# A two-layer graph attention kernel: when the second layer's softmax centre and weights are made, with deeper mask buffers and one product of the start held back

## The reference, cut to what matters

```python
src, dst = h @ a1, h @ a2
e = src[:, None] + dst[None, :]
e = where(e > 0, e, SLOPE * e)            # 0.01 in layer 0, 0.2 in layer 1
e = where(adj > 0, e, -9e15)
h_prime = softmax(e, axis=1) @ h
x = layernorm(x + h_prime)                # layer 1: h -> Wh = x @ W, and elu(h_prime)
```

## Time and profile before

| what | value |
|---|---|
| time, median of 3 runs | 433.5 us (432.94 to 433.63) |
| the profiled execution, its time | 433.0 us |
| its span, first to last instruction | 431.2 us |
| mean granted TensorE clock | 0.978 |
| PE busy | 397.9 us (92%) |
| DVE busy | 371.6 us (86%) |
| ACT busy | 382.6 us (89%) |
| POOL busy | 270.6 us (63%) |

### The profile page before, as it was taken

How to read it: one execution, slowest core, us unless ns; L and a number is a source line. 1 busy time by engine, 2 the same in 40 slices (tenths; PEclk the granted TensorE clock), 3 DMA queues, 4 the chain that set the end, 5 groups by cost and what they waited for, 6 DMA issues and landing times. The chain is left out here.

```text
span 431.2 us, 11604 instructions
## 1 busy us (share of the span) xinstructions
PE 397.9 (92%) x4372; PEld 385.7 (89%) x4372; DVE 371.6 (86%) x683; ACT 382.6 (89%) x594; POOL 270.6 (63%) x323
## 2 busy tenths in 40 slices
PE   3589999999999999999988999999999999999990
PEld 1478898899999999999887999999999999999980
DVE  4799999798899898998999978888888888888863
ACT  4789995998989898979999989999999999999920
POOL 5654287494967949497583226576766758493941
PEclk9599999999999999999999999999999999999995
DMA  6999959989999999999600000000000000000000
GB/s 123 97 104 104 83 41 91 96 62 101 83 96 99 86 96 74 96 81 91 56 14 2 2 26 2 2 26 2 27 2 24 0 24 0 24 2 26 2 26 16
DMA packets 38844, 21.66 MB, mean 50 GB/s; under 512 B 1808, under 2 KB 38800, under 8 KB 38800
## 3 DMA queue, kind: packets, MB, share of 16 engines
q0 software_dynamic: 33792, 16.78, 50.9%
q1 hardware_dynamic: 3920, 3.25, 2.5%
q10 hardware_dynamic: 1088, 1.05, 0.7%
HBM read 69.30 MB, written 2.10 MB: 166 GB/s over the span
## 5 line engine op out<-in xcount | busy, mean ns | idle before, releaser
L1254 PE MATMUL acc<-wmov,pos 128*128 128x195 bf16 x2016 | 357.0, 248 | 11.4 <-DVE pos L864 9.8
L673 ACT ACTIVATE neg<-srcb,dcol 128x512 int8<-128x512 f32 x512 | 357.0, 1014 | 0.5 <-PE acc L1254 0.3
L1254 PE MATMUL acc<-wmov,neg 128*128 128x195 bf16 x2016 | 357.0, 249 | 0.0
L1254 PEld LDWEIGHTS acc<-wmov,pos 128*128 128x128 fp8e5 x2016 | 198.6, 99 | 18.2 <-DVE pos L864 15.0
L1254 PEld LDWEIGHTS acc<-wmov,neg 128*128 128x128 fp8e5 x2016 | 197.6, 98 | 1.4 <-issue 0.7
L864 DVE SCALAR_TENSOR_TENSOR pos<-mask_t,neg 128x512 uint32<-128x512 uint32 x128 | 106.4, 831 | 23.1 <-PE acc L1254 11.0
L852 DVE SCALAR_TENSOR_TENSOR neg<-mask_t,neg 128x512 uint32<-128x512 uint32 x128 | 103.4, 808 | 10.5 <-ACT neg L673 9.2
L487 POOL DMA_DIRECT2D enc<-in_adj x64 | 49.3, 773 | 12.2 <-PE tb L1170 4.2
L349 POOL TENSOR_TENSOR scr<-scr,acol 128x260 f32<-128x260 f32 x14 | 13.3, 953 | 61.7 <-issue 51.8
L332 POOL TENSOR_TENSOR split<-val,bcol 128x520 f32<-128x520 f32 x15 | 17.6, 1174 | 26.9 <-DVE scr L396 12.2
L880 DVE TENSOR_REDUCE scr<-acc 128x130 f32<-128x390 f32 x60 | 31.6, 557 | 1.6 <-PE acc L1254 0.2
(11 more groups left out here) (138 smaller groups left out, 305.3 us busy)
## 6 DMA issues: line engine op xcount, KB each, us to landing
enc<-in_adj POOLq DMA_DIRECT2D x64, 256.0 KB, 11.5
x_chunks<-in_x ACTq DMA_DIRECT2D x4, 256.0 KB, 5.1
x_rows<-xout SPq DMA_DIRECT2D x8, 128.0 KB, 5.1
resid<-x_rows SPq DMA_DIRECT2D x8, 128.0 KB, 2.1
out<-xout SPq DMA_DIRECT2D x8, 128.0 KB, 1.7
resid<-in_a SPq DMA_DIRECT2D x1, 64.0 KB, 4.0
resid<-in_w SPq DMA_DIRECT2D x2, 16.0 KB, 4.0
att<-in_a SPq DMA_DIRECT2D x2, 0.2 KB, 4.5
```

The costliest lines, as they stand in the source:

```text
L673: ins = nc.scalar.activation(neg[:, k % SR, :, b], srcb[:, q % 2, :], ACT.Sign, bias=dcol[:, layer, c:c + 1])
L1254: ins = nc.tensor.matmul(acc[t][:, side * WC:(side + 1) * WC], m[:, t * P:(t + 1) * P, b], wmov[:, layer, c, side * WC:(side + 1) * WC], s ...
```

## The change

- The centre of layer 1 is the maximum over group 0 alone (`CENTRES = 1`), found in supertile 2 of layer 0. `centre` still cuts at +20, and the input check on the limits stays.
- From then on one group a supertile goes through the chain: group q - 2 is centred at DVE's step 4 of supertile q (step 1 in supertile 7) and exponentiated by ACT after its step 6 (step 4 in supertile 7); group q - 3 is multiplied by POOL after its stage 2, weighed by DVE at step 6 and kept by ACT after step 7, in supertiles 3 to 6. Supertile 7 weighs groups 4 and 5 (steps 4 and 6). Groups 6 and 7 stay in supertile 0 of layer 1.
- In supertiles 3 to 6 POOL's `multiply` stands ahead of the loads of step 3 and of `epilogue_norm`.
- The looks of supertiles 3 to 5 of layer 0 go: three are left in supertile 2, four in supertile 1 of layer 1, and five (before: four) in each of its supertiles 2 to 6.
- SR goes from 4 to 8 and MR from 2 to 4. The room comes from `s_prod` and `d_prod`, which now lie in the part of `mask_t` for supertiles 7 and 6.
- POOL's product for s waits until DVE has done all four products for d.
- The loop covers supertiles 3 to 6, and supertile 2 is written out; one semaphore replaces the pair `w_prod`.

The diff, cut to its core:

```diff
-SR = 4
-MR = 2
+SR = 8
+MR = 4
-EARLY = 5
+CENTRES = 1
-LOOKS = (4, 5)
-LATE_LOOKS = (2, 4, 5, 6)
-LATE = 12
+LOOKS = (3, 5, 6)
+LATE_LOOKS = (2, 4, 5, 6, 3)
+FEWER = 4
...
+        def spare(q):
+            return mask_t[:, q, :, :].rearrange("p u i -> p (u i)").bitcast(F32).rearrange("p (t d) -> p t d", d=F)
+
+        s_prod, d_prod = spare(NQ - 1), spare(NQ - 2)
...
                 body(layer, 0)
                 body(layer, 1)
+                body(layer, 2)
                 with eng.Fori(0, (NQ - 4) // 2) as i:
-                    body(layer, 2 * i + 2)
                     body(layer, 2 * i + 3)
-                body(layer, NQ - 2)
+                    body(layer, 2 * i + 4)
                 body(layer, NQ - 1)
...
             pool.wait_ge(x_landed[1], 16)
+            pool.wait_ge(d_mult, XP)
             nc.gpsimd.tensor_tensor(s_prod[:, TI:half], x_chunks[:, TI:half],
...
-                if layer == 0 and is_last_but_one(q):
-                    groups = {3: (0,), 5: (1,)}
-                if layer == 0 and is_last(q):
-                    groups = {3: (2,), 5: (3, 4, 5)}
+                if layer == 0 and not (is_first(q) or is_second(q) or is_third(q)):
+                    groups = {2: (q - 3,), 5: (q - 2,)} if is_last(q) else {2: (q - 3,)}
...
+            def exps_of_group(g, odd):
+
+                d, b = by_group(dcen), bcol[:, :, :].rearrange("p s (g b) -> p s g b", b=NB)[:, :, g]
+                act.wait_ge(dcen_set, g + 2)
+                apart(act, g)
+                nc.scalar.activation(b[:, 0], d[:, g], ACT.Exp)
+                nc.scalar.activation(b[:, 1], d[:, g], ACT.Exp, scale=SLOPE[1]).then_inc(b_set, 2 - odd)
+                if odd:
+                    even_out(b, b_lots(1, g) - 1, g)
...
-                    if layer == 0 and is_last_but_one(q):
-                        if k == 3:
-                            exps_of_d(1, 0, NB * EARLY, 1)
-                            even_out(weak_groups(0, EARLY), 5)
+                    if layer == 0 and not (is_first(q) or is_second(q) or is_last(q)):
                         if k == 6:
-                            keep_parts(1, 0)
+                            exps_of_group(q - 2, is_odd(q))
                     if layer == 0 and is_last(q):
                         if k == 4:
-                            exps_of_d(1, NB * EARLY, NB * (EARLY + 1), 2)
-                            even_out(weak_groups(EARLY, EARLY + 1), 8)
-                        if k == 6:
-                            keep_parts(1, 2)
+                            exps_of_group(q - 2, 1)
+                        if k == 5:
+                            keep_parts(1, q - 3)
...
                         if k == 2:
-                            exps_of_d(1, NB * (NQ - 2), NB * (NQ - 1), 3)
-                        if k in (0, 1, 6):
-                            keep_parts(1, {0: 4, 1: 5, 6: 6}[k])
+                            exps_of_group(NQ - 2, 0)
+                        if k in (0, 6):
+                            keep_parts(1, {0: 5, 6: 6}[k])
...
                         copy_turned(done[1])
-                        if is_last(q) or is_last_but_one(q):
-                            keep_parts(1, 3 if is_last(q) else 1)
+                        if not (is_second(q) or is_third(q) or is_last(q)):
+                            keep_parts(1, q - 3)
...
-                    if layer == 0 and is_last(q):
-
+                    if layer == 0 and is_third(q):
                         if k == 1:
-                            dve.wait_ge(grp_set, 3 * (EARLY + 1))
-                            centre(1, NB * EARLY, NB * (EARLY + 1))
-                        if k >= 4:
-                            weigh(1, k - 2)
-                    if layer == 0 and is_last_but_one(q):
-                        if k == 0:
-                            dve.wait_ge(grp_set, 3 * EARLY)
-                            find_max(1, NB * EARLY)
-                        if k == 1:
+                            dve.wait_ge(grp_set, 3 * CENTRES)
+                            find_max(1, NB * CENTRES)
+                        if k == 2:
                             spread_max(1)
-                        if k == 2:
+                        if k == 3:
                             take_max(1)
-                            centre(1, 0, NB * EARLY)
-                        if k in (4, 6):
-                            weigh(1, k // 2 - 2)
+                    if layer == 0 and not (is_first(q) or is_second(q)):
+                        if k == (1 if is_last(q) else 4):
+
+                            dve.wait_ge(grp_set, 3 * (q - 1))
+                            apart(dve, q)
+                            centre_group(q - 2)
+                        if k == (4 if is_last(q) else 6) and not is_third(q):
+                            weigh(1, q - 3)
+                        if k == 6 and is_last(q):
+                            weigh(1, q - 2)
...
-                        if layer == 0 and is_last_but_one(q) and k == 1:
+                        if layer == 0 and is_third(q) and k == 2:
                             spread_stat(1)
```

More of the change, by code:

```diff
@@ L40 @@
 MEAN_STEPS = (2, 4)
+SUMS = 0
 ALU = mybir.AluOpType
@@ L167, in fast_attention @@
         a_set = sem("a_set")
-        w_prod = [sem(f"w_prod{i}") for i in range(2)]
+        w_prod = sem("w_prod")
         w_vec = sem("w_vec")
@@ L208, in parts_of @@
         def parts_of(i):
-            return split[:, i % 2]
+            return split[:, is_odd(i)]
         def weights_of(layer, i):
-            g = i
-            return wmov[:, layer, NB * g:NB * g + NB]
+            return wmov[:, layer].rearrange("p (g b) c -> p g b c", b=NB)[:, i]
         def top_of(i):
@@ L255, in is_second, with is_third, is_odd @@
             return isinstance(q, int) and q == 1
-        def is_last_but_one(q):
-            return isinstance(q, int) and q == NQ - 2
+        def is_third(q):
+            return isinstance(q, int) and q == 2
         def is_last(q):
             return isinstance(q, int) and q == NQ - 1
+        def is_odd(q):
+            return int(q % 2)
         def all_supertiles(eng, body):
@@ L303, in b_lots @@
                 return 3 if is_weak(g) else 2
-            return 6 if g < EARLY else {EARLY: 9, EARLY + 1: 11, EARLY + 2: 14}[g]
+            return 3 + 2 * (g + 1)
         def s_lots(layer, q):
@@ L683, in body @@
                         group_values(NQ - 1)
-                        exps_of_d(1, NB * (NQ - 1), NB * NQ, 4)
-                        even_out(weak_groups(NQ - 1, NQ), 13)
+                        exps_of_group(NQ - 1, 1)
                     compare(layer, q, k)
@@ L691, in body @@
                             if k == 1:
-                                even_out(weak_groups(0, KB), 2)
+                                even_out(bcol[:, :, :].rearrange("p s (g b) -> p s g b", b=NB)[:, :, 1::2, :], 2)
                             keep_parts(0, k - 1)
@@ L794, in spread_max, with centre, centre_group @@
                 nc.vector.tensor_reduce(gst[0:1, 0:1], stat_bank(layer)[0:1, 0:P], AX.X, ALU.max).then_inc(gst_set, 1)
-            def centre(layer, c0, c1):
+            def centre(layer, dst, src):
                 dve.wait_ge(cmax_set, layer + 1)
-                nc.vector.tensor_scalar(dcen[:, c0:c1], dcol[:, layer, c0:c1], cmax[:, layer, 0:1], ABOVE,
+                nc.vector.tensor_scalar(dst, src, cmax[:, layer, 0:1], ABOVE,
                                         ALU.subtract, ALU.min).then_inc(dcen_set, 1)
+            def centre_group(g):
+                centre(1, by_group(dcen)[:, g], by_group(dcol[:, 1, :])[:, g])
             def take_max(layer):
@@ L900, in find_limits @@
             def find_limits(layer):
-                dve.wait_ge(dcen_set, 5 if layer else 1)
+                dve.wait_ge(dcen_set, NQ + 1 if layer else 1)
                 for i, op in enumerate((ALU.min, ALU.max)):
@@ L967, in _ @@
             take_max(0)
-            centre(0, 0, KB * NB)
+            centre(0, dcen[:, :], dcol[:, 0, :])
             extract_single(0)
@@ L1018, in body @@
                     positive(layer, q, k)
-                    if done is not None and k == 0:
+                    if done is not None and k == SUMS:
                         sum_parts(*done, range(0, TI // 2))
@@ L1035, in body @@
                             take_stats(*done)
-                    if layer == 0 and not (is_first(q) or is_second(q) or is_last_but_one(q) or is_last(q)):
-                        if k in LOOKS:
-                            look(2 * q - 4 + LOOKS.index(k), pieces(1, NU - 1))
+                    if layer == 0 and is_third(q) and k in LOOKS:
+                        look(LOOKS.index(k), pieces(1, NU - 1))
                     if layer == 1 and not is_first(q):
-                        if k in LATE_LOOKS and not is_last(q):
-                            look(4 * q + LATE - 8 + LATE_LOOKS.index(k), pieces(NQ - 1, NU - 1))
```

(8 more changed lines are left out.)

23 lines of the change are left out of this document (11 added, 12 removed).

## The result

| | before | after |
|---|---|---|
| median | 433.24 us (4 runs, 432.94 to 433.63) | 428.78 us (4 runs, 428.51 to 429.21) |
| ratio after/before | | 0.9898, 95% interval 0.988 to 0.9915 |
| profiled execution, its time | 433.0 us | 428.54 us |
| span | 431.2 us | 426.9 us |

What follows compares the result with a forecast made beforehand. PE's products alone bound it from layer 1's supertile 2 on; earlier, PE waits for `pos` and d's maximum. Terms -1.4 + 0.7 + 0.4 - 1.65 - 2.5 - 0.4 = -4.85 us gave 428.6 us, range 425.5 to 431.8.

Steps and rivals of the forecast that it cites:

- What bounds the kernel: From layer 1's supertile 2 on PE's products alone, 22.59 us a supertile; before it, PE's waits can be won.
- 0/6, 0/7: Supertiles 6 and 7 of layer 0: DVE relieved of weights work, -1.65 us and -2.5 us.
- The start: Holding POOL's product for s shortens DVE's fourth d product; 1.4 us won and kept.
- 0/2: Supertile 2 of layer 0: DVE's maximum, `centre` and extra look plus PE's two small instructions cost +0.7 us.
- 0/3 to 0/5: Supertiles 3 to 5 of layer 0: DVE and ACT exactly full; PE stalls 0, 0.2 and 0.2 us.
- the first rival: Hand-overs between ACT and DVE in layer 0's supertiles 4 to 7 take 2.6 us back: 431.2 us; chance 0.20.
- The buffers: Layer 0's supertiles 3 to 5: deeper buffers help the unevenness little, as DVE and ACT wait at every supertile's edge.
- 1/0: Supertile 0 of layer 1: group 7's chain stays, only DVE's lateness from the supertile before goes, -0.4 of 1.5 us.
- 1/1 and 1/2: Supertiles 1 and 2 of layer 1: the first unchanged, the second's extra look hidden by DVE's free time.
- The buffers' case: Rival: buffers even out everything in layer 0 and layer 1's supertile 0; 424.2 us, half way 426; chance 0.17.
- The hand-over between ACT and DVE: The first rival: ACT waits for `weigh`, starts the next supertile late, DVE's signs and sums come late; chance 0.20.
- the slower case: Rival: POOL's `multiply` ahead of the norm delays `turn_group` and stops PE over four supertiles; 434.5 us; chance 0.06.

Runs made afterwards that it cites:

- run 1: The kernel before with the hold alone (POOL's product for s waits for all four products for d): 431.96 us against 433.19, ratio 0.9969.
- run 2: The changed kernel without the hold of POOL's product for s at the start: 430.06 us, ratio 0.9917 to the kernel before.
- run 9: The changed kernel, unaltered, timed and profiled once more: 428.36 us against 433.38 for the kernel before, ratio 0.9885.
- run 7: The changed kernel with two looks back in each of layer 0's supertiles 3 to 6, none in supertile 2: 431.63 us, ratio 0.9952.
- run 8: The changed kernel with POOL's `multiply` behind the loads of step 3 in layer 0's supertiles 3 to 6: 430.73 us, ratio 0.9932.
- run 3: The kernel before with the deeper buffers alone (SR 8, MR 4): 433.87 us against 433.19, ratio 1.0012.
- run 4: The changed kernel with the shallow buffers (SR 4, MR 2): 428.48 us, ratio 0.9883 to the kernel before.
- run 5: The changed kernel with ACT keeping group 4's parts after step 6, not 5, of layer 0's supertile 7: 428.22 us, ratio 0.9869.
- run 10: As run 5, and ACT copies turned group 7 ahead of keeping group 6's parts in layer 1's supertile 0: 426.95 us, ratio 0.9848.

## Why the prediction came out

- **What bounds the kernel**: right. From 1/2 on, PE's products alone; the gain is where PE waited, in 0/6, 0/7 and the start.
- **The start**: right in mechanism and size, 1.4 forecast, 1.34 alone (run 1), 1.36 taken away (run 2, against run 9). All of it reaches the end: in run 1 no later supertile changes.
- **0/2**: the terms were right, the total was not, +0.7 forecast, +0.2 measured. PE pays 0.41 in step 2 for the maximum's two instructions (3.64 to 4.05; 0.4 was put) and 0.33 in step 3 (2.77 to 3.10; 0.3 was put), which is the look there: without looks in 0/2 step 3 is back at 2.77 (run 7). What I did not put is that steps 0 and 1 get 0.59 shorter (3.64 and 3.34 to 3.50 and 2.89). What shortens them was not tested.
- **0/3 to 0/5**: the total was right, its working partly. That DVE is exactly full is shown by run 7. The hold-up by `multiply` that I averaged to 0.35 is 0 at its place in 0/4 and 0.68 where it comes 1.6 us later, which run 8 shows. The Trainium skill ("SBUF — State Buffer", "SBUF: two separate sides") has this as an exclusive lock between GpSimd and DVE instructions with two SBUF inputs; the traces agree, with `pos` stretched from 0.69 to 1.37 and the statistics, one input each, not. My text called this lock at its full 1.5 us the first rival, but the sum of that rival is worked out without it. The 0.4 all lie in 0/5, not 0.2 each in 0/4 and 0/5, and PE has no wait of its own named there. ACT waits for `weigh` at the end of 0/4, and DVE's first `neg` for 0/5 comes late (its wait at the same place before 0/4 is 0.71):

```profile
147.95 1.07 ACT L646 COPY wmov<-split 128x1040 bf16 x1 [0.82 <-DVE split L851]
```

```profile
152.05 0.69 DVE L865 SCALAR_TENSOR_TENSOR neg<-mask_t,neg 128x512 uint32<-128x512 uint32 x1 [1.07 <-ACT neg L688]
```

- **The buffers**: right that they give nothing, and shown from both sides (runs 3 and 4); run 3's 0.7 us stay open.
- **0/6, 0/7**: right, -4.15 forecast, -4.5 measured; the stall left before step 5 is 1.36, from the `weigh` in step 4, as put. ACT's `keep_parts` one step behind its `weigh` waits for it, as I wrote, and this is where my text stopped too early.
- **1/0, the step that failed**: "only what DVE brings in late from 0/7 goes: -0.4". I took 1/0 for bound by DVE and by group 7's chain. What the runs show in its place: ACT's list from 0/7 to group 7's copy is the bound. ACT's wait of 1.65 in 0/7, over at 218.27, comes out 25 us later as PE's stall of 0.63 before step 4 of 1/0 (243.14), and 0.94 us of keeping parts stand ahead of the copy that starts group 7's chain. Without the wait 1/0 is 0.8 shorter (run 5), with the copy first another 0.9 (run 10), together 24.25, below the 24.77 of before and near my 24.4. The stall in steps 6 and 7, which I said would stay, stayed.
- **1/1 and 1/2**: I said unchanged; they won 0.58, and do so in every variant of the changed kernel, with either buffers and without the hold. The traces show an order that turned. At the end of 1/1 a DVE `neg` meets a POOL instruction of the epilogue (L412, in the changed kernel L420). In the kernel before, and in runs 1 and 3, POOL's starts first, by 0.02 to 0.04 us, and `neg` lasts 1.12 to 1.14 us (POOL's 0.61). In the changed kernel and all its variants `neg` starts first, by 0.05 to 0.1, and lasts 0.69 (POOL's 1.07 to 1.11). Behind it come DVE's sums, which in the chain that ended last of the kernel before release PE's first product of 1/2. That this is the whole of the 0.58 was not tested. 1/3 gives 0.13 to 0.20 back in every variant; it does so in run 7 too, which has four looks in it as before, so it is not the fifth look.
- **The rivals**: no PE wait came from POOL's `xout`, and the slower case stayed away (its own sum, four times 1.4 on 428.6, is 434.2, not 434.5). The buffers' case is excluded by run 3. The hand-over between ACT and DVE was real: ACT waits for `weigh` 0.60, 0.82, 0.62 and 0.82 in 0/3 to 0/6, and 1.65 in 0/7. It goes with PE time in only two places, the 0.4 of 0/5 and, shown by run 5, the 0.8 of 1/0, and so takes 1.2 and not 2.6.

The forecast of the total was helped by errors that cancel: 1.5 too much hoped for in 1/0 and 0.6 in the first profile's start, against 0.5 in 0/2, 0.4 in 0/6 and 0/7 and 0.7 in the supertiles that I left unchanged.

## What to carry to other kernels

Where three engines are nearly full, follow each one's list through the whole stretch, not supertile by supertile: a wait of ACT that cost nothing where it stood came out 25 us later, and the same work in another order gave 1.4 us. Buffers twice as deep gave nothing here, to either kernel; measure them alone before giving them memory. An instruction on POOL has a price that depends on what DVE does in that microsecond, so its place matters even when nobody waits for its result.

## What was not expected of the hardware

- A `multiply` of 1.07 us on POOL costs PE nothing at one place in 0/4 and, 1.6 us later in the same step order, 0.3 to 0.7 us in each of 0/3 to 0/6 (run 8), with `pos` at 0.69 and 1.37.
- Which of two such instructions is stretched turned on less than 0.1 us: at the end of 1/1 it is DVE's `neg` (1.12 against 0.69) where POOL's starts 0.04 before it, and POOL's (1.08 against 0.61) where `neg` starts 0.09 before it.
- The granted clock has a half-speed stretch near the start (0.50 of 2.4 GHz, so 1.2 GHz), and its place varies between executions. In the kernel before it holds PE's first products; in run 10 it comes later, after 2 us in which PE stood still. The kernel before, then run 10:

```profile
18.00:22.00 4.00, 2.66 (x17) 2.14 (x16) 3.35 (x6) 4.00 (x8) 2.61 (x4) 0.50 1.24 103
```

```profile
22.00:24.00 2.00, 0.00 (x0) 0.01 (x1) 1.97 (x4) 2.00 (x4) 0.05 (x1) 0.99 1.24 103
24.00:26.00 2.00, 2.00 (x13) 1.86 (x14) 1.97 (x3) 0.66 (x2) 1.07 (x1) 0.50 1.25 104
```

The same window in run 5 and in run 9, with PE's instructions in it (x50 and x72):

```profile
22.00:30.00 8.00, 6.00 (x50) 5.78 (x51) 7.84 (x11) 6.18 (x9) 3.36 (x5) 0.79 1.24 105
```

```profile
22.00:30.00 8.00, 6.51 (x72) 6.04 (x70) 7.83 (x12) 6.32 (x10) 3.68 (x5) 1.00 1.24 103
```

0/0 lasted 33.48 and 32.88 in them, though their code is alike there. It is so in all thirteen profiles: in the five with the stretch behind 24 us (runs 2, 3, 5, 8 and 10) 0/0 lasts 33.32 to 33.49, in the others 32.88 to 32.97. The recorded clock does not show every such stretch: in run 9 the first products begin 0.16 us apart, as in the kernel before at 0.50, and 0.09 apart after that, with 1.00 recorded up to 52 us. Half a microsecond between two profiles of this kernel can be this alone, so small edits are better judged by the supertiles behind it.
